# A Mamba layer and a routed expert layer on one core: centred output weights, and the work between them reordered

## The reference, cut to what matters

```python
# x: (2, 2048, 128), all float32
def mamba(x):                                   # d_inner 256, d_state 16, 4 taps
    h = (x - mean(x)) / sqrt(var(x) + 1e-6) * gamma + beta
    u, z = split(h @ in_proj_w.T)
    uc = silu(causal_conv4(u) + conv_b)
    dt, Bm, Cm = split(uc @ x_proj_w.T)
    delta = softplus(dt @ dt_proj_w.T + dt_proj_b)
    state = exp(delta * A) * state + delta * Bm * uc      # along the sequence
    y = (sum_n(state * Cm) + uc * D) * silu(z)
    return y @ out_proj_w.T + x
def ffn(x):                                     # 8 experts, the best 2 of each row
    p, i = top_k(softmax(x @ Wg + bg), 2)
    e(x) = gelu(x @ W1[e] + b1[e]) @ W2[e] + b2[e]
    return p[0] * e_i0(x) + p[1] * e_i1(x)
x = layernorm(x + mamba(x))
x = layernorm(x + ffn(x))
```

## Time and profile before

| | us |
|---|---|
| median of 3 executions (lowest, highest) | 779.25 (778.39, 782.07) |
| the profiled execution, its own time | 782.08 |
| its span, from the first to the last instruction | 780.3 |
| mean granted TensorE clock (1.0 is 2.4 GHz) | 0.898 |
| busy: VectorE, TensorE, GpSimd, ScalarE | 662.5, 602.2, 577.6, 434.3 |
| first scan starts, last scan starts | 42.2, 558.6 |
| first expert tile on TensorE | 601.66 |

### The profile page before, as it was taken

How to read it: one execution, slowest core, us unless ns; L and a number is a source line. 1 busy time by engine, 2 the same in 40 slices (tenths; PEclk the granted TensorE clock), 3 DMA queues, 4 the chain that set the end, 5 groups by cost and what they waited for, 6 DMA issues and landing times. The chain is left out here.

```text
span 780.3 us, 11886 instructions
## 1 busy us (share of the span) xinstructions
PE 602.2 (77%) x3071; PEld 293.7 (38%) x3071; DVE 662.5 (85%) x1343; ACT 434.3 (56%) x892; POOL 577.6 (74%) x544
## 2 busy tenths in 40 slices
PE   9768888987987888898798676685431999999920
PEld 4322222322322322232232122121131999998920
DVE  4288999999999999999998999999633788886855
ACT  3758587578467576657746644334110656554625
POOL 4345787976999899899899989968765456664644
PEclk9889999999999999999999987767755999999975
DMA  3095386577669668657656764954003677776754
GB/s 94 17 226 136 81 188 162 122 164 160 142 158 256 138 150 202 144 122 180 145 135 140 164 155 103 209 127 104 25 29 114 183 204 203 216 209 171 197 166 175
DMA packets 51169, 117.34 MB, mean 150 GB/s; under 512 B 8816, under 2 KB 25008, under 8 KB 43040
## 3 DMA queue, kind: packets, MB, share of 16 engines
q1 hardware_dynamic: 45344, 107.20, 56.4%
q0 software_dynamic: 4320, 8.99, 3.6%
q10 hardware_dynamic: 1440, 0.40, 0.2%
HBM read 100.21 MB, written 16.35 MB: 149 GB/s over the span
## 5 line engine op out<-in xcount | busy, mean ns | idle before, releaser
L554 POOL TENSOR_TENSOR hc<-hs,Crep 128x1024 f32<-128x1024 f32 x128 | 301.1, 2359 | 72.3 <-DVE hs L1395 51.3
L1395 DVE TENSOR_TENSOR_SCAN hs<-bank,state,flow 128x512 f32<-128x512 f32 x256 | 312.8, 1267 | 15.7 <-ACT bank L1136 7.5
L1136 ACT ACTIVATE bank<-bank,negA 128x512 f32<-128x512 f32 x256 | 164.6, 660 | 168.2 <-PE bank L805 158.8
L805 PE MATMUL bank<-delta,sel 64*128 64x512 f32 x512 | 157.5, 694 | 85.5 <-DVE hs L1395 83.6
L1378 DVE TENSOR_TENSOR flow<-flow,bank 128x2048 f32<-128x2048 f32 x63 | 142.8, 2266 | 0.0
L1279 ACT ACTIVATE flow<-bank,b1T 128x128 f32<-128x128 f32 x284 | 81.2, 369 | 58.0 <-issue 31.1
L805 PEld LDWEIGHTS bank<-delta,sel 64*128 64x128 f32 x512 | 42.3, 201 | 179.0 <-DVE hs L1395 149.3
L680 POOL DMA_INDIRECT results<-flow,idn x71 | 70.0, 985 | 33.1 <-issue 31.3
L814 PE MATMUL bank<-hc,kc 128*32 128x512 f32 x512 | 73.2, 646 | 10.8 <-POOL hc L554 10.8
L995 PE MATMUL bank<-flow 128*128 128x128 f32 x568 | 78.6, 283 | 1.9 <-DVE flow L1546 1.6
L1003 PE MATMUL bank<-w_sb,flow 128*128 x568 | 76.0, 277 | 1.6 <-ACT flow L1279 1.3
(11 more groups left out here) (198 smaller groups left out, 806.3 us busy)
## 6 DMA issues: line engine op xcount, KB each, us to landing
flow<-du_d SPq DMA_DIRECT2D x63, 1024.0 KB
flow<-L_ffn_W SPq DMA_DIRECT2D x71, 256.0 KB
xg<-xs SPq DMA_DIRECT2D x71, 66.0 KB
du_d<-du SPq DMA_DIRECT2D x28, 128.0 KB
xin<-L_attn_x SPq DMA_DIRECT2D x8, 256.0 KB, 3.3
hs<-results SPq DMA_DIRECT2D x8, 256.0 KB, 4.4
out<-hc SPq DMA_DIRECT2D x8, 256.0 KB, 2.0
results<-flow,idn POOLq DMA_INDIRECT x71
```

What stands on the lines that cost most here:

```text
L554: nc.gpsimd.tensor_tensor(hc[:, Q % 2, two, :], hs[:, Q % 2, two, :], Crep[u % 3][:].unsqueeze(1).broadcast_to([P, 2, T]), ALU.mult).then_ ...
L805: ins = nc.tensor.matmul(dbank[2 * odd + i][:], sel[rows, odd, q % 4, :], delta[u % 2][rows, q // 4, :])
L1136: nc.scalar.activation(dbank[G % 4][:], dbank[G % 4][:], ACT.Exp, scale=negA[:, ch:ch + 1]).then_inc(s_ex, 1)
L1395: nc.vector.tensor_tensor_scan(hs[:, Q % 2, j, :], dbank[G % 4][:], flow[Q % 3][:, j, :], state[:, Q // QUADS % 2, Q % QUADS, j:j + 1], AL ...
```

## The change

- The output weights are centred once, in unit 0: the mean over the 128 output columns is taken from each row of `woutT`. The output product then has mean 0, and the LayerNorm's input 2x + y W has twice the mean of x, which the front statistics know already.
- For units 0 to 6 TensorE adds 2x in the output product itself, with a matrix of 2 on the diagonal (`twice`), ScalarE copies the sum from PSUM to `res` (step 17) and squares it with the known mean as bias and a sum over the row (steps 18 and 19), and GpSimd makes the standard deviation from that sum (`back_spread`, slot 7). Unit 7 keeps the former residual and statistics.
- `negative_part` moves from step 19 to 21, `xns` from 22 to 24, `xnT_evac` from 25 to 27, `xn_T` from 25 to 26, `logits` from 28 to 29, `best_two` from 29 to 30, the last unit's `one_hots` from 30 to 31, a half of `proj_x` from 29 to 30.
- In unit 7 the rows are listed in slots 8 to 11 instead of 11 to 14.
- In the tail: `post` stands ahead of ranks and places of unit 6; `tag_rows` is split, and `name_rows` stands ahead of the masks; 5, 30 and 64 matmuls of ones stand ahead of `out_proj`, ahead of `xn_T` and behind the last ranks; ScalarE runs one Gelu on a scrap tile behind its last `gate_exp`.

```diff
-KEPT_BUSY = {..., 25: (4, "xn", -1), 27: (6, "xn", -1)}
-DRAINED_BY_DVE = {(w, u) for w in ("out", "logits", "ranks") for u in range(UNITS)} | {("T", 1), ("u0", 1)}
+KEPT_BUSY = {..., 26: (4, "xn", -1), 28: (4, "xn", -1)}
+DRAINED_BY_DVE = {(w, u) for w in ("logits", "ranks") for u in range(UNITS)} | {("out", UNITS - 1)} | {("T", 1), ("u0", 1)}
...
@@ GpSimd
             def front_rstd(u):
                 pool.wait_ge(s_fag, u + 1)
                 after(pool, s_xh, u)
+                nc.gpsimd.tensor_scalar(twice_minus[:, u, :], mv[:, :, 0], -2.0, None, ALU.mult).then_inc(s_tm, 1)
                 rsqrt(veps, rstd, nmean, nmr, mv, 1e-6, s_frs, u)
+            def back_spread(u):
+                pool.wait_ge(s_sq, u + 1)
+                after(pool, s_xn, u)
+                nc.gpsimd.tensor_scalar(cveps[:], squares[:], 1.0 / D, 1e-5, ALU.mult, ALU.add).then_inc(s_crs, 2)
+                pool.wait_ge(s_crs, 4 * u + 2)
+                nc.gpsimd.tensor_tensor(crstd[:], cveps[:], minus_half[:], ALU.pow).then_inc(s_crs, 1)
+                pool.wait_ge(s_crs, 4 * u + 3)
+                pool.wait_ge(s_tm, u + 1)
+                nc.gpsimd.tensor_tensor(cnmr[:], twice_minus[:, u, :], crstd[:], ALU.mult).then_inc(s_crs, 1)
-            def tag_rows(u):
+            def name_rows(u):
                 pool.wait_ge(s_xn, u + 1)
-                pool.wait_ge(s_er, u + 1)
                 pool.wait_ge(s_ti, u + 1)
...
+            def weigh_rows(u):
+                pool.wait_ge(s_er, u + 1)
...
+                    if slot == 7 and j >= 1:
+                        back_spread(j - 1)
-                            tag_rows(j - 2)
-                        if slot in (11, 12, 13, 14):
+                            name_rows(j - 2)
+                            weigh_rows(j - 2)
+                        listing = (11, 12, 13, 14) if late else (8, 9, 10, 11)
+                        if slot in listing:
...
-                    if slot == 8 and j >= 1:
-                        back_rstd(j - 1)
...
+            nc.gpsimd.tensor_tensor(twice[:], ident[:], ident[:], ALU.add).then_inc(s_tw, 1)
...
             shift_ex(last - 1)
+            name_rows(last - 1)
             mask_ranks(last - 1)
             places(last - 1)
-            tag_rows(last - 1)
+            weigh_rows(last - 1)
...
             shift_ex(last)
+            name_rows(last)
             mask_ranks(last)
             places(last)
-            tag_rows(last)
+            weigh_rows(last)
@@ TensorE
                 for t in ts:
                     for h in range(HALVES):
                         ins = nc.tensor.matmul(mbank[:, P * t:P * t + P], yg[:, h, P * t:P * t + P], woutT[:, h, :],
-                                               start=(h == 0), stop=(h == 1))
+                                               start=(h == 0), stop=(h == 1 and u == UNITS - 1))
+                    if u < UNITS - 1:
+                        ins = nc.tensor.matmul(mbank[:, P * t:P * t + P], twice[:], xin[u % 4][:, t, :], start=False, stop=True)
...
+            def idle_tail(times):
+                for _ in range(times):
+                    nc.tensor.matmul(dbank[3][:], ones[:], idle_rhs[:])
...
             ranks(last - 1)
+            idle_tail(5)
             out_proj(last, (0, 1, 2, 3))
+            idle_tail(30)
             xn_T(last)
             logits(last)
             ranks(last)
+            idle_tail(64)
@@ ScalarE
+            def residual(u):
+                after(act, s_xn, u)
+                nc.scalar.copy(res[:].rearrange("p t d -> p (t d)"), filled(u, "out")[:]).then_inc(s_fd, 1)
+            def squared(u, ts):
+                if ts[0] == 0:
+                    drained(act, fill_of(u, "out"))
+                    act.wait_ge(s_tm, u + 1)
+                    after(act, s_crs, 4 * u)
+                for t in ts:
+                    ins = nc.scalar.activation(square[:, t, :], res[:, t, :], ACT.Square, bias=twice_minus[:, u, t:t + 1],
+                                               accum_out=squares[:, t:t + 1])
+                if TT - 1 in ts:
+                    ins.then_inc(s_sq, 1)
...
+                    if g == 17 and j >= 1:
+                        residual(j - 1)
+                    if g in (18, 19) and j >= 1:
+                        squared(j - 1, ((0, 1), (2, 3))[g - 18])
...
             gate_exp(last)
+            act.wait_ge(s_scrap, 2)
+            nc.scalar.activation(scrap[:], minus_half[:], ACT.Gelu).then_inc(s_scrap, 1)
@@ VectorE
+            def centre_weights():
+                dve.wait_ge(s_pe, 6)
+                nc.vector.reduce_sum(wsum[:], woutT[:], AX_X).then_inc(s_wc, 1)
+                dve.wait_ge(s_wc, 1)
+                nc.vector.tensor_scalar(wsum[:], wsum[:], -1.0 / D, None, ALU.mult).then_inc(s_wc, 1)
+                dve.wait_ge(s_wc, 2)
+                nc.vector.tensor_tensor(woutT[:], woutT[:], wsum[:].unsqueeze(2).broadcast_to([P, HALVES, D]), ALU.add)\
+                    .then_inc(s_wc, 1)
...
-                    if g == 16 and j >= 1:
-                        residual(j - 1)
-                    if g == 17 and j >= 1:
-                        back_stats(j - 1)
+                    if g == 9 and j == 0:
+                        centre_weights()
...
-            ranks(last - 1)
-            place(last - 1)
             post(last, 1)
+            ranks(last - 1)
+            place(last - 1)
             residual(last)
             back_stats(last)
```

More of the change, by code:

```diff
@@ L59 @@
 FILLS = fill_order()
-KEPT_BUSY = {3: (4, "dt1", 1), 15: (3, "out", -1), 19: (6, "u1", 2), 23: (3, "z0", 2), 25: (4, "xn", -1), 27: (6, "xn", -1)}
-DRAINED_BY_DVE = {(w, u) for w in ("out", "logits", "ranks") for u in range(UNITS)} | {("T", 1), ("u0", 1)}
+KEPT_BUSY = {3: (4, "dt1", 1), 15: (3, "out", -1), 19: (6, "u1", 2), 23: (3, "z0", 2), 26: (4, "xn", -1), 28: (4, "xn", -1)}
+DRAINED_BY_DVE = {(w, u) for w in ("logits", "ranks") for u in range(UNITS)} | {("out", UNITS - 1)} | {("T", 1), ("u0", 1)}
 def fill_of(u, what):
@@ L168, in mamba_moe @@
         cst = sb("cst", [P, TT, 6])
+        twice = sb("twice", [P, P])
+        wsum = sb("wsum", [P, HALVES])
+        twice_minus = sb("twice_minus", [P, UNITS, TT])
+        squares = sb("squares", [P, TT])
+        square = sb("square", [P, TT, D])
         cmv = sb("cmv", [P, TT, 2])
@@ L302, in mamba_moe @@
         s_cag = sem("ln1_aggr")
+        s_tw = sem("two_on_the_diagonal")
+        s_wc = sem("output_weights_centred")
+        s_tm = sem("twice_minus_mean")
+        s_sq = sem("ln1_squares")
         s_crs = sem("ln1_rstd")
@@ L825, in out_proj @@
                     pe.wait_ge(s_yd, 2 * u + 2)
+                if u == 0 and 0 in ts:
+                    pe.wait_ge(s_wc, 3)
+                    pe.wait_ge(s_tw, 1)
                 for t in ts:
@@ L1186, in host @@
                             minus_linear(j + 1)
-                        if g == 19:
+                        if g == 21:
                             negative_part(j + 1)
@@ L1415, in back_stats @@
                 after(dve, s_crs, 4 * u)
-                moments(cst, res, cmv, s_cst, s_cag, u)
+                moments(cst, res, cmv, s_cst, s_cag, 0)
             def best_two(u):
@@ L1494, in host @@
                         front_stats(j + 3)
-                    if g == 29 and j >= 1:
+                    if g == 30 and j >= 1:
                         best_two(j - 1)
-                    if g == 30 and j == UNITS - 1:
+                    if g == 31 and j == UNITS - 1:
                         one_hots(j - 1)
@@ L1507, in _ @@
             last = UNITS - 1
+            post(last, 1)
             ranks(last - 1)
             place(last - 1)
-            post(last, 1)
             residual(last)
```

16 lines of the change are left out of this document (8 added, 8 removed).

## The result

The changed kernel takes 773.31 us (median of 9 runs, 771.38 to 777.49) beside 781.71 for the kernel before on the same chip: ratio 0.9906, interval 0.9884 to 0.9929. The ratio makes the gain 7.3 us, the two medians 8.4; I go by the ratio. A second set of six runs on another occasion gave 0.9906 again (0.9881 to 0.9932). The forecast was 15.4 us less, and still 8.25 at the slow end of its range: the sign is right, the size half, and 773.31 lies outside the range (758.5 to 771). The profiled execution took 773.31 (span 771.4, 8.9 shorter than before's).

What follows compares the result with a forecast made beforehand. VectorE, nearly full in the Mamba units (19.75 of 20 us), was taken as the bound until GpSimd's 2.5 us of waits ran out. Units 9.4 + tail 3.6 + tile start 2.4 = 15.4 us: 763.9 against the median, range 758.5 to 771.

Steps and rivals of the forecast that it cites:

- rival B: ScalarE's squares need another table, two loads (5.1 us) per unit; time 783.5 to 786; chance 0.06.
- 6 x 1.76 - 1.2 = 9.4 us: Units 1 to 6: VectorE saves 1.76 us each, less 1.2 us of waits for GpSimd at four boundaries.
- GpSimd's 1.40 us before scan 4: Unit boundary: hc product ends 310.76, scan 4 starts 312.16; the 1.40 us between was read as slack.
- The check by sums: Per unit: GpSimd's work 62.6 us against VectorE's need afterwards of 63.3 us, so "it just fits".
- waits for scans: GpSimd, in a 65.05 us unit window, waits 2.5 us for scans; VectorE's savings count until these run out.
- Rival A: GpSimd becomes the bound in the units; host gain 5 us, time 768; chance 0.15.
- D: Nothing measurable: order effects eat the units' gain, idle products the tail's; time 777; chance 0.05.
- moving the listing so takes no work away: Unit 7, slots 8 to 11: the move only makes GpSimd late earlier; the unit's gain is 1.5 us.
- Chain and tile start: Last hc product to tile 0: 3.6 us sooner, unit 7's 1.5 included; tile 0's first products: gain 2.4 us.
- the thirty: Idle products ahead of xn_T: 6.5 us at the higher clock, ending 576.0, 0.4 us late.
- The sixty-four: Idle products ahead of tile 0: 13.9 us from 580.8, ending 594.7, and fit before tile 0 at 598.1.
- Rival C: Tail's idle products run at 1.2 GHz; tile 0 near 616, time 783; chance 0.04.

Runs made afterwards that it cites:

- after_again: The changed kernel itself, unedited, run and traced a second time: ratio 0.9906 to the kernel before.
- after_part1: Changed kernel without the tail's idle products, Gelu, unit 7's listing move and the new places of post, name_rows and last one_hots: ratio 0.9966 to the kernel before.
- lockfree_row_means: Changed kernel with gate bias added in PSUM, one-hots compared from PSUM, three small front LayerNorm instructions moved from GpSimd to ScalarE: 761.79 us, ratio 0.9748.
- experiment 4: Changed kernel, one_hots before scan 0, plus four idle products in step 5 (0.9853), three GpSimd instructions on ScalarE (0.9906), both (0.9969); idle products on changed kernel alone: 0.9966.
- after_list11: Changed kernel with the last unit's listing back in slots 11 to 14: ratio 0.9893 to the kernel before.
- before_oh3: Kernel before with one_hots(j-2) called behind scan 3 instead of scan 0: ratio 1.0388 to the kernel before.

## Why the prediction was half right

**The work moved as forecast.** Between the gated output of one unit's step 7 and of its step 23 the kernel is faster by 1.77 us in unit 1 (1.76 forecast: yg at 122.98 and 155.05 before, 122.64 and 152.93 after), and by 1.76 to 1.77 in units 2, 5, 6 and 7; the stretch up to the next step 7 then gives 1.6 to 2.4 of it back at four of six boundaries. The squares took 393 ns for 369, plus 190 for reading the accumulator, but with both they follow each other 0.38 to 0.40 us apart, so the 0.2 us for the accumulator were hardly needed. No table was loaded for them: rival B is out. GpSimd waited for them 0.74 us in unit 1 and 0.89 in unit 7 (0.7 forecast there), and not in between.

**The step that failed** is the sum of units 1 to 6, "6 x 1.76 - 1.2 = 9.4 us": it let VectorE's saving through at every boundary, and took GpSimd's 1.40 us before scan 4 for slack. Measured is nothing. From the end of unit 0's slot 15 to the end of unit 6's the kernel before takes 391.98 us and the changed one 392.00; unit 1 gives 1.7 and unit 2 0.2, units 3 and 4 cost 0.8 and 2.5, units 5 and 6 give 0.3 and 1.1. Five more traces with the same units (after_again, after_part1 and the three that leave out a piece of the chain) lie at 391.2 to 392.4. In the kernel before the unit was already bound by a loop that leaves steps 16 and 17 out: GpSimd from slot 4 to slot 15 (53.1), the 1.41 that the lock adds, VectorE from scan 4 through scan 9 up to the first product behind it (10.51), together 65.05, the period of the rows. The check by sums (62.6 for GpSimd, 63.3 for VectorE, "it just fits") added each engine's work by itself and so could not see a loop that passes from one to the other. The evidence was in the rows: a gap of 1.4 us at four boundaries, equal to a hundredth or two, is what a common trigger leaves, not slack between two engines that run on their own. Of the 2.5 us that GpSimd "waits for scans", 2.02 lie ahead of slot 4 and are VectorE's part of that loop; they don't run out when VectorE gets faster elsewhere. That units 3 and 4 even lost comes from the second stretch, 0.6 and 2.0 us longer. TensorE's clock in the window 304 to 312 (PE, PEld, DVE, ACT, POOL busy, clock, DMA share, GB/s), after then before:

```profile
304.00:312.00 8.00, 5.73 (x24) 2.13 (x24) 7.88 (x7) 3.61 (x5) 7.50 (x6) 0.62 0.53 134
```

```profile
304.00:312.00 8.00, 5.90 (x40) 2.13 (x32) 7.97 (x7) 5.71 (x10) 7.50 (x5) 1.00 0.65 163
```

TensorE had stood idle 3.33 us for the scans behind the blocked comparison, and its groups of four products then took 2.08 us for 1.13; decays came late by up to 1.20 us. In lockfree_row_means, where the clock did not fall, the second stretch is 10.51 again. The idle time alone does not set the loss: at the boundary to unit 5 TensorE stood idle 3.54 us in the changed kernel and the second stretch is still 10.51, since the clock came back sooner. Scan 0 to slot 4 of units 4 and 5:

```profile
300.94:323.38 22.44, 17.49 (x71) 5.38 (x72) 20.38 (x17) 14.92 (x22) 17.59 (x13) 0.77 0.63 148
368.52:389.12 20.60, 14.83 (x71) 4.54 (x72) 20.35 (x18) 15.13 (x25) 17.78 (x13) 0.92 0.68 156
```

In other traces of the same units the 2 us fell on unit 5, or on none, so the 2.5 us of unit 4 are partly this execution's. That idle products help here was not shown: those of experiment 4 mended one boundary and made two worse.

**Rival A**, GpSimd as the bound (chance 0.15, 768 us, 11.3 less than before), was nearest to the 7.3 measured: right in the engine, for a reason it didn't name, and too short in its price, as it still gave the units 5 us. It should have been the forecast, with the lock in the loop. D, no gain at all (777), was right on the units and wrong on the tail. B's own terms (5.7 and 2.4 more, 4.5 less) make 782.9 and not 783.5 to 786; nothing hangs on it.

**Unit 7** gave 3.2 us for 1.5 forecast. The reasoning "moving the listing so takes no work away" missed that GpSimd waited for scans in slots 8 to 11 (1.57 us and 0.27 in its timeline) and that the issues fill those waits: up to 1.4 us by after_list11. Without that move unit 7 gives 1.8 (57.99 for 59.78 in after_part1), near the 1.5. In the second trace unit 7 gave 2.2 and not 3.2. `one_hots` behind the last scan is held 5.02 us, and ends (559.69) with the last hc product (559.59), so it cost nothing, as said.

**Chain and tile start**: 2.1 us (3.6 less unit 7's 1.5) plus 2.4 were forecast, 4.5 in all; from the last hc product to the first output product the first trace has 3.6 us, and the second (39.5 for 44.2) 4.7. Near, and mostly by its own terms: the thirty ran at the higher level (0.22 us each) and did not delay xn_T (it still waited 0.78 us for xn), tile 0 started at clock 1.00, and its stretch fell by 2.1. The sixty-four began at the lower level (granted 0.50 up to 582 us) and took 15.76 us for the 13.9 forecast, but fitted all the same: they end at 594.4, tile 0 follows at 596.57. Rival C is out but for that start.

**Summed up**: units 1 to 6 gave 0.0 us for 9.4, unit 7 3.2 for 1.5, chain and tile start 3.6 for 4.5, 0.3 came ahead of unit 1 and 1.7 from tiles that were not edited: 8.9 of span. The range's slow end had still allowed 5 us for the units. That half of the forecast gain arrived is luck in part: the term that carried most of it gave nothing, and unit 7 and the unedited tiles gave 3.4 us more than was counted on.

## What to carry to other kernels

Before a saving on a full engine is counted once per iteration, close the loop: write the iteration's time as a sum of stretches, each with the engine that sets it, and see whether the instructions you remove lie in one. A gap that is the same to a hundredth or two of a microsecond at every boundary may be no slack but a coupling; look for a small instruction in front of it whose duration varies, here from 0.2 to 2.8 us. It was VectorE reading two SBUF tensors beside GpSimd. Giving it one operand from PSUM, and making the sum behind it a reduction, freed it here; do that before anything around it is tuned, since in this kernel even an improvement (0.9 us less on GpSimd) was answered by the lock with a loss.

## What the runs showed of the hardware

A two-input VectorE instruction that loses to GpSimd is held until GpSimd's whole run of back-to-back products is over (5.0 to 7.2 us in before_oh3, in front of or within runs of three that take 6.9), and not only until the current one ends; a stretch of indirect DMA issues lets it through (0.20 to 0.22 us). With one operand from PSUM the comparison takes 0.18 us inside an hc product too. ScalarE's square with an accumulator is two instructions, 393 and 190 ns, that overlap to 0.38 to 0.40 us a pair; 28 of them between Exps brought no table load.
